# Three scan-stage steps move in a hand-written order: a convolution, the cumulated sums, the exponents

## The reference, cut to what matters

```python
zxbcdt = xn @ W_in.T                        # 256 gates z, 320 channels xBC, 8 step sizes dt
xBC = silu(conv4(xBC) + conv_b)             # causal convolution of 4 taps along the tokens
xs, Bm, Cm = split(xBC)                     # 256 + 32 + 32
dt = softplus(dt + dt_bias); dA = exp(dt * -exp(A_log))
state = state * dA + (dt * x) B             # scan over the tokens, 8 heads
y = state . C + Dp * xs
x + rmsnorm(y * silu(z)) @ W_out.T
```

## Time and profile before

| What | Value |
|---|---|
| Runs, us | 954.06, 957.86, 958.05 (median 957.86) |
| Profiled execution, us | 954.08 |
| Its span, us | 952.3 |
| Busy share of the span: PE, DVE, ACT, POOL | 90%, 76%, 53%, 31% |
| Mean granted clock of the TensorE | 0.969 of full |

### The profile page before, as it was taken

One profiled execution on the slowest core, in us unless ns is written; L12 is line 12 of the kernel. 1 busy time (PEld: TensorE's weight loads), 2 busy tenths in 40 slices (PEclk: granted clock), 3 DMA queues, 4 the chain that ended last, 5 costly groups with the idle time before them and its releaser, 6 DMA issues.

```text
span 952.3 us, 18728 instructions
## 1 busy us (share of the span) xinstructions
PE 858.4 (90%) x7086; PEld 670.9 (70%) x7086; DVE 724.0 (76%) x1959; ACT 503.3 (53%) x740; POOL 290.8 (31%) x264
## 2 busy tenths in 40 slices
PE   3788999999998869898989899899789999999997
PEld 2555556656665758686868777776578898888887
DVE  2867677678767686868687787977968889888885
ACT  1524455455557457566575757464335544555453
POOL 0026110110010236354545454647530333033300
PEclk9979999999999879899999999999899999999999
DMA  5641011011100303213030303041000000000001
GB/s 150 192 143 23 1 23 23 1 23 23 23 1 0 77 4 74 48 31 71 8 76 3 78 1 78 1 96 50 2 1 1 24 23 24 1 23 23 24 2 44
DMA packets 30888, 36.07 MB, mean 38 GB/s; under 512 B 4560, under 2 KB 24912, under 8 KB 30800
## 3 DMA queue, kind: packets, MB, share of 16 engines
q1 hardware_dynamic: 29648, 30.68, 13.2%
q10 hardware_dynamic: 1152, 4.19, 1.2%
HBM read 21.50 MB, written 4.98 MB: 28 GB/s over the span
## 4 chain that ended last, share of the span: by engine, by line
PE 58%; DVE 27%; ACT 7%; issue 5%; POOL 2%; SPq 0%; DMA 0%; DVEq 0%; POOLq 0%; ACTq 0%
PE ps L1047 7%; PE ps L715 6%; DVE cacc L1713 5%; DVE acc L1997 5%; PE ps L702 4%; PE ps L794 3%; PE ps L969 3%; PE ps L796 3%; PE ps L669 3%; PE ps L795 3%; PE ps L674 2%; PE ps L691 2%; PE ps L905 2%; PE ps L684 2%; PE ps L919 2%
## 5 line engine op out<-in xcount | busy, mean ns | idle before, releaser
L1997 DVE SCALAR_TENSOR_TENSOR acc<-ps,comb,acc 128x128 f32<-128x128 f32 x512 | 139.8, 343 | 16.2 <-PE ps L1047 15.6
L1400 ACT ACTIVATE hid<-ps,b_f 128x512 f32<-128x512 f32 x128 | 87.2, 687 | 112.2 <-PE ps L796 112.1
L1047 PEld LDWEIGHTS ps<-w_f,hid 128*128 128x128 f32 x1024 | 130.6, 191 | 19.5 <-ACT hid L1400 8.0
L1047 PE MATMUL ps<-w_f,hid 128*128 128x128 f32 x1024 | 136.8, 277 | 5.0 <-ACT hid L1400 4.5
L1570 DVE TENSOR_REDUCE nmax<-ps 128x1 f32<-128x1024 f32 x64 | 78.1, 1220 | 29.7 <-PE ps L674 29.4
L1713 DVE SCALAR_TENSOR_TENSOR cacc<-ps,cw,cacc 128x1023 f32<-128x1023 f32 (+5 forms) x72 | 91.8, 1275 | 9.4 <-ACT cacc L1272 7.7
L1341 ACT ACTIVATE dcy<-ps 128x1024 f32<-128x1024 f32 x64 | 65.2, 1018 | 62.4 <-PE ps L919 62.3
L570 POOL TENSOR_TENSOR srs<-sve,neg_half 128x1 f32<-128x1 f32 x64 | 58.4, 912 | 117.7 <-DVE gram L1822 117.6
L1187 ACT ACTIVATE probs<-ps,nmax 128x1024 f32<-128x1024 f32 x64 | 71.3, 1113 | 39.2 <-DVE nmax L1570 36.5
L1805 DVE SCALAR_TENSOR_TENSOR dcy<-dcy,g_sb 128x1024 f32<-128x1024 f32 x64 | 85.4, 1334 | 0.3
L702 PEld LDWEIGHTS ps<-id_f,probs 128*128 128x128 f32 x512 | 59.0, 142 | 33.0 <-issue 23.3
(11 more groups left out here) (214 smaller groups left out, 1865.3 us busy)
## 6 DMA issues: line engine op xcount, KB each, us to landing
c_dec<-exp_dram SPq DMA_DIRECT2D x32, 256.0 KB, 5.4
xc<-in_x SPq DMA_DIRECT2D x8, 512.0 KB, 3.6
q_b<-q_a SPq DMA_DIRECT2D x16, 256.0 KB, 2.8
X<-in_x_tok ACTq DMA_DIRECT2D x8, 512.0 KB, 5.3
c_rep<-cacc SPq DMA_DIRECT2D x32, 128.0 KB, 4.6
out<-o_ch SPq DMA_DIRECT2D x8, 512.0 KB, 2.6
w_f<-in_w SPq DMA_DIRECT2D x2, 512.0 KB, 4.1
cst_f<-in_sel_rows SPq DMA_DIRECT2D x1, 512.0 KB, 4.4
```

What stands on the lines that cost most here:

```text
L1047: last = nc.tensor.matmul(ps[:, Y_BANKS[n], t * P:(t + 1) * P], hid[n % 2][:, t * P:(t + 1) * P], w2_f[:, e, :], start=True, stop=True)
L1400: nc.scalar.activation(hid[n % 2][:], ps[:, 4 + n % 2, :], ACT.Gelu, bias=b1_f[:, n // 2:n // 2 + 1]).then_inc(e_hidden_ready, 1)
L1997: done = nc.vector.scalar_tensor_tensor(acc[u][:, tt, :], ps[:, bank, t * P:(t + 1) * P], comb[u][:, tt, e:e + 1], acc[u][:, tt, :], ALU.m ...
```

## The change

Seven entries of the hand-written lists get another slot. No instruction is added or removed, and no code outside the lists changes.

```diff
-   (group, (2, 1), 2, 5.5), (cumulate, (), 2, 6.5)]
+   (group, (2, 1), 2, 5.5), (cumulate, (), 2, 7)]
...
-   (shortcut, (4, NT), 1, 5.5), (factors, (), 2, 7)]
+   (shortcut, (4, NT), 1, 5.5), (factors, (), 2, 7.5)]
...
-   dve_parts = [("conv", (2, 2), 1, -0.25), ("conv", (2, 3), 1, 0), ("ends", (), 1, 1), ("low", (), 2, 2.75),
+   dve_parts = [("conv", (2, 3), 1, -0.25), ("ends", (), 1, 1), ("low", (), 2, 2.75),
                 ("inner", (), 1, 3), ("conv", (0, 1), 2, 4), ("conv", (0, 2), 2, 4), ("conv", (0, 3), 2, 4),
-                ("steps", (), 2, 4.5), ("conv", (1, 1), 2, 5), ("conv", (1, 2), 2, 5),
-                ("softplus", (0,), 2, 5.5), ("softplus", (1,), 2, 5.5), ("conv", (1, 3), 2, 6),
-                ("exponents", (), 2, 7), ("conv", (2, 1), 2, 7)]
+                ("steps", (), 2, 4.5), ("conv", (1, 1), 2, 5), ("conv", (1, 2), 2, 5), ("conv", (1, 3), 2, 5),
+                ("softplus", (0,), 2, 5.5), ("softplus", (1,), 2, 5.5), ("conv", (2, 1), 2, 6),
+                ("conv", (2, 2), 2, 7), ("exponents", (), 2, 7.5)]
```

More of the change, by code:

```diff
@@ L1014, in _ @@
                         (steps, (0, 4), 2, 3.5), (turn_b, (), 1, 3.5), (steps, (4, NT), 2, 4), (group, (1, 0), 2, 4.5),
-                        (group, (1, 1), 2, 4.5), (group, (2, 0), 2, 5.5), (group, (2, 1), 2, 5.5), (cumulate, (), 2, 6.5)]
+                        (group, (1, 1), 2, 4.5), (group, (2, 0), 2, 5.5), (group, (2, 1), 2, 5.5), (cumulate, (), 2, 7)]
             def pieces(b, slot):
```

## The result

The kernel after takes 974.8 us (median of 4 runs, 970.25 to 977.38), the one before 956.75 (4 runs): ratio 1.0187, 95% interval 1.0136 to 1.0239. It is slower, by 18 us. The forecast was 972, range 961 to 982.

What follows compares the result with a forecast made beforehand. DVE and PE were the busy engines, with the turns' chain of waits also through ACT. Delay 10.3 plus clock 6.5 made 16.8 us: 970.9 on the profiled 954.08, 974.7 on the median; forecast 972, range 961 to 982.

Steps and rivals of the forecast that it cites:

- DVE, step by step: On DVE in chunk 7, two convolutions (1.27 us each) and gated rows (0.55) put the exponents 3.09 us later.
- A turn costs 1.7 us: Each of five like turns between scans grows 1.7 us, through late factors on ACT and PE's decay.
- The first turn's 1.8: Delay taken for the first turn, whose slots differ: near the middle of 1.27 to 2.54 us.
- The stall that goes: PE's 2.13 us wait ahead of the cumulated sums goes, but some 3.2 us return ahead of the gates: no gain.
- The clock: PE's longer idle time ahead of the gates lowers its clock: 1.3 us a turn, 6.5 us for five.
- The reading behind the clock: PE's clock stayed at 1.00 behind 2.13 us idle and was 0.50 behind 4.83; 3.2 us lies between.
- What I cost at nothing: Late gated rows, POOL's roots and SP's row DMAs were taken to add 0 us.
- (a): Rival: PE's clock falls in full at every turn, 5 x 2.65 us, giving 977.7 us; chance 0.24.
- (b): Rival: ACT or a later wait takes up the delay, turns keep their length, 954 to 958 us; chance 0.09.
- (c): Rival: removing PE's stall ahead of the cumulated sums carries through to the gates, 1.25 us a turn, 946.6 us; chance 0.09.

Runs made afterwards that it cites:

- the filler: Kernel after, plus four extra PE products that nobody reads, ahead of the gates in all six turns: 964.7 us, ratio 1.0077.
- the last version: Kernel before, with the change's chunk 5 and 6 convolutions, exponents ahead of the mixed tile, POOL's operand ahead of its root, cumulated sums behind decay: 953.4 us, ratio 0.9963.

## Why the prediction was right, point by point

- *DVE, step by step*: right. 0.55 us from the gated rows to the exponents and 0.65 to their last instruction stand in the rows after as worked out; in the turn with full clock the exponents start 24.98 us into it against 21.87 before, 3.11 later for 3.09. The idle time of ACT is 5.82 us ("over 5").
- *A turn costs 1.7 us*: 1.6 measured on turns with full clock, 1.2 on the first turn where 1.8 was taken; together 9.2 us for 10.3. The first turn's 1.8 was the mis-sized one.
- *The stall that goes*: right; 3.34 us ahead of the gates for 3.2, and nothing won by it.
- *The clock*: 6.5 us forecast as a middle between 0 and 2.65 a turn; 8.5 net in the profiled execution. The mechanism held, but that the sum comes so near is in part luck. No turn behaves like the mean: one of the five lost nothing, and two lost over 4 us, so that they came out 5.6 us and more longer where "up to 4" was forecast. Their second fall lies some 6 us into the turn, away from the gates, and was not in the sum; two of them cost about 3.1 us, by the 47.49 - 45.93 = 1.56 of the filler. Nor was the clock in it that turns of before had lost already, 2.95 us. The two nearly cancel; the falls at the gates alone cost about 8.3.
- *The reading behind the clock*: that 2.13 us of idle time "alone did not do it" holds for the one turn read. In the turn of 45.77 us, in the same trace, the same stall ahead of the sums (2.15 us, ended at 436.67) was followed by a granted clock of 0.50 from 438.5 to 441.8 us. So 2.13 was no safe end of the interpolation.
- *What I cost at nothing*: one sentence was wrong, that only DVE's `output` waits for POOL's roots. The next operand queues behind them. In the kernel after it does not show, since the gates are later still; it is 0.7 us a turn once they are not.
- *Rivals*: (a), a full fall at every turn, did not come, though the clock fell at or behind the gates in four of five; with 4.54 us of idle time (the experiment with one more convolution) it fell there in all. (b) and (c) fell with the wait at the gates; the last version shows where (c) would have held.

## What to carry to other kernels

A wait that an order removes pays only if the next thing due is early too: ask for each moved step what stands behind it on its own engine, and behind the waiters of that. A reserve (1.28 us here) is used up by the sum of the moves, and it holds only for the wait at which it was read: other waits that the moves reach (POOL's operand, DVE's `output`) have their own, and a queue on an idle engine belongs to the reckoning. Compare stretches with equal granted clock first; then price the clock by itself, by giving the idle engine something to do, and look where else in the kernel that brings back clock.

## What was not expected of the hardware

The clock also fell in a stretch without idle time: in the kernel before, PE was busy all of 466 to 472 us, and the granted clock went from 1.00 to 0.50. (Its last idle time, 0.33 us, had ended at 464.20.) Just ahead of the fall, from 465.66 to 468.5 us, PE ran sixteen products of 16 columns (L843, L844), eight of 32 (L895) and the two wide ones of a `decay`. Three windows follow; the columns are window, length, PE busy (count), PE clock, DMA share, GB/s.

```profile
466.00:468.00 2.00, 2.00 (x20) 1.00 0.00 0
468.00:470.00 2.00, 2.00 (x12) 0.79 0.00 0
470.00:472.00 2.00, 2.00 (x24) 0.50 0.00 0
```

The same place cost two turns their clock in the kernel after (one of the two falls of the turns of 50.10 and 49.95) and three with the filler. Over the eleven traces it is 20 of 55 like turns; in the others the same products ran and the clock held. What decides was not tried, nor whether the narrow products are the cause.
